# A state-space and expert kernel: the unrolled middle chunks of the first stage become hardware loops

## What is computed

```python
xz = einsum('bld,ed->ble', x, in_proj_w); xi, z = split(xz)          # 512 each
u  = silu(causal_depthwise_conv4(xi) + conv1d_b)
dt_low, B, C = split(einsum('bld,rd->blr', u, x_proj_w))             # 16, 16, 16
delta = softplus(dt_low @ dt_proj_w.T + dt_proj_b)
dA, dBu = exp(delta[..., None] * A), delta[..., None] * B * u[..., None]
h_t = dA_t * h_{t-1} + dBu_t ;  y_t = sum_n h_t[..., n] * C_t[n]     # 16 states
x1 = layernorm(x + ((y + u * D) * silu(z)) @ out_proj_w.T)
# then: softmax router over 8 experts, each expert takes its 2048 best tokens,
# layer norm, two-layer GELU network, weighted scatter-add, and a last layer norm
```

## Time and profile before

| | us |
|---|---|
| three runs | 4682.22, 4683.41, 4690.44; median 4683.41 |
| the profiled execution | 4683.41 |
| its span, first to last instruction | 4681.5 |
| mean granted clock of TensorE, share of full | 0.883 |

### The profile page before, as it was taken

The page is one execution under the profiler, slowest core; times in us unless marked ns, Lnnn a source line. Parts: engine busy times, 40 slices in busy tenths (PEclk is TensorE's granted clock), DMA queues, the critical chain, the costliest instruction groups (busy, mean ns, idle before and its releaser), DMA issues. The chain is left out here.

```text
span 4681.5 us, 57838 instructions
## 1 busy us (share of the span) xinstructions
PE 3739.5 (80%) x19154; PEld 2596.0 (55%) x19154; DVE 3996.9 (85%) x5099; ACT 3393.0 (72%) x5732; POOL 3574.0 (76%) x1744
## 2 busy tenths in 40 slices
PE   7888888888888888888888878888863199999990
PEld 3455555555555555555555555555553178888880
DVE  4999999999999999999999999999994667766645
ACT  5888787888888888878887888888861056555555
POOL 3888888888888888888888888888881156666643
PEclk8889898989888988988898998989875599999995
DMA  2454555554445545545554445545442123333328
GB/s 69 118 127 126 127 125 132 126 127 126 117 122 138 133 120 133 126 117 127 134 130 125 121 119 133 137 122 136 124 112 48 50 46 64 70 60 62 63 33 291
DMA packets 166374, 528.78 MB, mean 113 GB/s; under 512 B 31920, under 2 KB 97584, under 8 KB 118720
## 3 DMA queue, kind: packets, MB, share of 16 engines
q0 software_dynamic: 56832, 268.99, 29.5%
q1 hardware_dynamic: 104640, 239.32, 14.8%
q10 hardware_dynamic: 4608, 16.78, 0.9%
HBM read 221.47 MB, written 68.68 MB: 62 GB/s over the span
## 5 line engine op out<-in xcount | busy, mean ns | idle before, releaser
L369 POOL TENSOR_TENSOR dbu<-du,bb 128x2048 f32<-128x2048 f32 x512 | 2361.8, 4634 | 298.8 <-DVE h L736 274.0
L736 DVE TENSOR_TENSOR_SCAN h<-da,hlast,dbu 128x512 f32<-128x512 f32 x1536 | 1881.4, 1267 | 53.0 <-POOL dbu L369 41.9
L656 PE MATMUL ht<-ident,h 128*128 128x128 f32 x8192 | 1320.7, 308 | 594.6 <-DVE h L736 347.2
L419 ACT ACTIVATE da<-dl,negA 128x512 f32<-128x512 f32 x2048 | 1418.7, 698 | 468.9 <-DVE h L736 463.3
L656 PEld LDWEIGHTS ht<-ident,h 128*128 128x128 f32 x8192 | 1042.5, 157 | 1075.9 <-DVE h L736 555.2
L744 DVE SCALAR_TENSOR_TENSOR pair<-ht,ct,pair 128x512 f32<-128x512 f32 x896 | 639.0, 731 | 85.8 <-PE ht L656 85.4
L736 DVE TENSOR_TENSOR_SCAN h<-da,dbu 128x512 f32<-128x512 f32 x512 | 596.1, 1205 | 39.8 <-ACT da L419 25.0
L442 ACT ACTIVATE pair<-ht,ct 128x512 f32<-128x512 f32 x896 | 591.8, 687 | 50.7 <-PE ht L656 48.4
L589 PE MATMUL spare<-xin,win 128*128 128x512 f32 x1024 | 499.2, 617 | 40.3 <-DMA xin<-in_xt 26.0
L595 PE MATMUL spare<-xh,conv 128*128 128x512 f32 x1024 | 460.8, 592 | 2.2 <-ACT dl L456 1.5
L1149 POOL DMA_INDIRECT sums<-ot,idx x128 | 237.2, 1853 | 172.3 <-DVE ot L1425 130.7
(11 more groups left out here) (162 smaller groups left out, 5688.3 us busy)
## 6 DMA issues: line engine op xcount, KB each, us to landing
acc<-pair POOLq DMA_DIRECT2D x224, 1024.0 KB, 7.1
bb<-b_rows SPq DMA_DIRECT2D x128, 1024.0 KB, 5.2
xin<-in_xt SPq DMA_DIRECT2D x32, 512.0 KB, 4.4
xres<-in_x SPq DMA_DIRECT2D x32, 512.0 KB, 4.1
x_scores<-xres SPq DMA_DIRECT2D x32, 512.0 KB, 5.4
sums<-xres SPq DMA_DIRECT2D x32, 512.0 KB, 7.1
wraw<-in_w SPq DMA_DIRECT2D x16, 1024.0 KB
rows<-sums SPq DMA_DIRECT2D x32, 512.0 KB, 6.3
```

What stands on the lines that cost most here:

```text
L369: pool.tensor_tensor(dbu[n % 2][:], du[q][:], bb[part % 2][:, m:m + 1, :].to_broadcast([P, DT, CH]), ALU.mult).then_inc(dbu_done, 1)
L419: act.activation(da[DA_SLOT[m]][:], dl[q][:, dt, :], ACT.Exp, scale=negA[:, dt, n:n + 1]).then_inc(exp_done, 1)
L656: last = te.transpose(ht[HT_SLOT[m]][:, dt * P:(dt + 1) * P], h[n % 2][:, dt, b * P:(b + 1) * P], ident[:])
L736: dve.tensor_tensor_scan(h[n % 2][:, dt, :], da[DA_SLOT[n * DT + dt]][:], dbu[n % 2][:, dt, :], start, ALU.mult, ALU.add).then_inc(scan_do ...
```

## The change

In each of the five engines' blocks of `stage1` the Python loop over chunks 2 to 29 becomes a hardware loop, `Fori`. On SP, ACT and PE a turn of the loop is two chunks, and there are 14 turns; on POOL and DVE a turn is four chunks, and there are 7. The longer turn is needed since these two treat a sequence's first chunk in another way. Inside the loop the chunk's number is made from the loop's register, so the counts of the waits and the addresses that contain it are computed by register operations when the program runs. No other line changes.

```diff
 # SP (ACT and PE alike)
-                for c in range(2, n_chunks - 2):
-                    chunk(c, c % 2, (FR, P1, P2), True)
+                with sp.Fori(1, n_chunks // 2 - 1) as j:
+                    chunk(2 * j, 0, (FR, P1, P2), True)
+                    chunk(2 * j + 1, 1, (FR, P1, P2), True)
 # POOL (DVE alike)
-                for c in range(2, n_chunks - 2):
-                    chunk(c, c % 4, (FR, P1, P2), True)
+                with pool.Fori(0, n_chunks // 4 - 1) as j:
+                    chunk(4 * j + 2, 2, (FR, P1, P2), True)
+                    chunk(4 * j + 3, 3, (FR, P1, P2), True)
+                    chunk(4 * j + 4, 0, (FR, P1, P2), True)
+                    chunk(4 * j + 5, 1, (FR, P1, P2), True)
```

More of the change, by code:

```diff
@@ L561, in _ @@
                 chunk(1, 1, (FR, P1))
-                for c in range(2, n_chunks - 2):
-                    chunk(c, c % 2, (FR, P1, P2))
+                with act.Fori(1, n_chunks // 2 - 1) as j:
+                    chunk(2 * j, 0, (FR, P1, P2))
+                    chunk(2 * j + 1, 1, (FR, P1, P2))
                 chunk(n_chunks - 2, 0, (FR, P1, P2))
@@ L700, in _ @@
                 chunk(1, 1, (FR, P1), (FR,), True)
-                for c in range(2, n_chunks - 2):
-                    chunk(c, c % 2, (FR, P1, P2), (FR, P1, P2), True)
+                with te.Fori(1, n_chunks // 2 - 1) as j:
+                    chunk(2 * j, 0, (FR, P1, P2), (FR, P1, P2), True)
+                    chunk(2 * j + 1, 1, (FR, P1, P2), (FR, P1, P2), True)
                 chunk(n_chunks - 2, 0, (FR, P1, P2), (FR, P1, P2), False)
@@ L823, in _ @@
                 chunk(1, 1, (FR, P1))
-                for c in range(2, n_chunks - 2):
-                    chunk(c, c % 4, (FR, P1, P2))
+                with dve.Fori(0, n_chunks // 4 - 1) as j:
+                    chunk(4 * j + 2, 2, (FR, P1, P2))
+                    chunk(4 * j + 3, 3, (FR, P1, P2))
+                    chunk(4 * j + 4, 0, (FR, P1, P2))
+                    chunk(4 * j + 5, 1, (FR, P1, P2))
                 chunk(n_chunks - 2, 2, (FR, P1, P2))
```

## The result

The kernel with the loops takes 4820.94 us (median of four runs, 4809.72 to 4828.28) against 4684.05 us before (four runs, 4682.22 to 4690.44). The ratio is 1.0288, with a 95% interval of 1.0264 to 1.0311: 2.9% slower, 137 us. The sign was forecast, the size was not: 4727 us was predicted, and 4821 lies above the range of 4700 to 4785. The profiled execution of the changed kernel took 4813.78 us, its span is 4812.0.

A forecast was written before the change was run, and what follows sets the result against it. The prediction took DVE to bound the kernel and added 38 us for ACT's jumps, 3 for PE's and 3 for registers: 4683.4 + 44 = 4727 us, 0.9% slower. The range was 4700 to 4785 us.

The forecast's parts named there:

- What bounds the kernel: In the state-space stage DVE sets the pace, at 108.5 us a chunk, idling for 6% of it.
- PE's jump: At 13 turn ends PE jumps back, late by 0 to about 1 us and mostly covered: 3 us.
- rival 3: PE's jump at turn ends comes on top of ACT's: 36 us in place of 3, 4760 us; chance 0.13.
- ACT's jump, "the main term": At 13 turn ends a 4.5 us jump delays the first decay, exposing 2.8 or 3.25 us: 38 us.
- lower working: The estimate for ACT's 13 jumps with DVE's 2.9 us in place of 4.5: 17 us.
- DVE's and POOL's jumps: Six each, at turn ends, hidden under ACT's delay: nothing; uncovered, 1.5 us a time for DVE, up to 2.5 for POOL.
- Registers, 3 us: Register operations for waits and addresses in the looped chunks add 0.1 us a chunk, 3 us.
- The equal groups of the expert stage: Four groups there took 100.60 us unrolled, 100.03 and 100.57 looped, taken to show no register cost that can be told.
- the upper bound of 365 us: All some 170 DVE register operations a chunk on the path at about 78 ns: 13 us a chunk.
- rival 4: Register operations stand on DVE's path: a tenth of 365 us gives 4761, a third 4846; above 4790, chance 0.05.
- The sum: Over the looped chunks, ACT's jump 38, PE's jump 3 and registers 3 make 44 us.

The follow-up runs named there:

- padded kernel: The kernel before with the loop on PE alone, plus 12 transposes of the identity (24 instructions) ahead of PE's work: 4707.08 us, ratio 1.0043.
- middle-of-a-block kernel: The changed kernel with 71 transposes (142 instructions) ahead of PE's work, so its loop's head stands mid-block: 4736.51 us, ratio 1.0113 to the kernel before.

## Why the prediction was wrong in size

**What bounds the kernel** was right. DVE's work is unchanged, and what the kernel lost is its idle time.

**PE's jump: the step that failed.** "I take 3 us, as PE may not pay at all and mostly has cover." It did pay, 3.3 to 5.0 us a jump, with 1842 instructions of all kinds in the turn. That it mostly has cover held for the jump alone (20 to 23 us in the padded kernel, registers of PE included). What was missing is the second stop. The target is 14 instructions ahead of a packet's end, PE uses them up in its fifth transpose, and stands for 1.9 to 6.5 us before the next. This is rival 3's way (PE late, passed on whole) with another size: it had 2.8 us a jump, 36 in all, and PE measured 81 to 86 alone and 96 to 101 within the change (4821 against 4725). In the expert stage PE stood for 2.55 us where the group took 4.0 us longer; the prediction noted that this was not all of it, and did not follow it further. PE does not stop a second time there, so that loop could not have shown what was missing.

The Trainium skill (Runtime: NRT & Kernel Launch, Instruction fetch mechanics) says that the stream comes in 16 KiB blocks, fetched in sequence ahead of use, and that crossing a block's boundary is mostly hidden. PE's packets here have that size, those of q14 have 1.94 MB / 238 = 8 KB. Hidden it was in the unrolled kernel, where no transpose of PE is behind a stop of "issue", and not behind a jump, where 5.68 us were seen. The page also gives PE's memory for instructions as 2048 of them, though it speaks of a window of two blocks beside it; the body of 1842 was not held, as each of the 13 jumps took 3.3 us and more. It is the measurement that decides here.

**Why the next packet is late** is in part argued. In the changed kernel three of PE's packets start around the first jump (branch at 507.3): at 508.0, 508.4 and 516.5 us. I take the first for the sequential successor of the loop's end, which is of no use after the jump, and the second for the target. The loop's end lies some 36 instructions into a packet, so that the fetch ahead and the jump can meet. At the six jumps without such an extra packet the next one starts 0.7 to 1.5 us behind the branch's end, and PE goes on 2.2 to 3.3 us after that start. So it comes only once the target runs, and 14 instructions do not last that long. Seven of the 13 jumps have the extra packet. In five of them it starts at most 0.9 us ahead of the target's, and these are the five longest second stops, 5.68 to 6.50 us; the other two have 2.35 and 3.46, and the six jumps without one 1.87 to 3.07. In the five the awaited packet starts 4.4 to 5.1 us behind the branch's end. So the second stop is there with and without the extra packet, and long where the two start together. In the middle-of-a-block kernel, where the loop's end lies elsewhere too, there is no such packet and its jumps are 3.3 to 3.9 us. Two kernels moved the loop's end alone, by another length of the turn: with turns of four the end is some 86 instructions into a packet and the six second stops are 2.25 to 2.86 us, with turns of twelve it is 15 to 30 into one, the two packets start 0.4 us apart, and the one second stop is 5.39 us. So the head's place brings the stop, and the end's place seems to decide whether it is a long one; the head was never moved alone.

**How ACT passes it on** is read from the timelines: its product waits 5.84 us for the tile and the decays stand behind it. That the wait comes with PE's loop and goes with its second stop is shown (DVE's waits on `da` 84.8 us with PE's loop alone, 29.9 with it padded, 23.2 before). That putting decays ahead of that product would save the time wasn't tried. Beside this, PE's clock was at its lower level for the stretch: 0.51 from 514 to 524 us against 1.00 from 500 to 514. It fell while PE stood, and eleven transposes behind the stop took 2.50 us where twelve took 1.47 at 526 us.

```profile
500.00:514.00 14.00, 8.94 (x35) 4.51 (x34) 10.66 (x12) 7.97 (x15) 9.22 (x4) 1.00 0.59 121
514.00:524.00 10.00, 5.16 (x15) 3.60 (x15) 3.02 (x3) 4.32 (x9) 3.16 (x2) 0.51 0.28 57
```

That makes the second stop's harm somewhat larger than its length; how much of it was not separated.

**ACT's jump, "the main term".** The mechanism was right, where it was said to be: a decay late at a turn's first scan. The term of 38 us was mis-sized, by taking 4.5 us from the expert stage. The jump took 2.5 to 3.6 us here, DVE's waits for a decay at the turns' first scans are 23.6 us in the changed kernel, and ACT's loop alone cost 13 to 15 us. The prediction's lower working, 17 us with 2.9 us a jump, was near.

**DVE's and POOL's jumps, nothing as they lie under ACT's.** POOL's 6 us alone fits nothing to little. DVE's loop measured 30 alone, of which some 16 are registers, so 14 for six jumps without cover, or 11 by the idle time at their scans; 9 were said. Within the change they cannot be told from the rest.

**Registers, 3 us.** They are about 27, 1 us a chunk. The equal groups of the expert stage were a poor witness, as the prediction half said: PE was the bound there, so DVE's spare time can have taken them up. A tenth of the upper bound of 365 us (rival 4) was nearer than 0.1 us a chunk.

**The sum.** By the single parts: PE 81 to 86, DVE 30, ACT 13 to 15, POOL 6. Seen by kinds: about 27 of registers, 60 to 77 of PE's second stop, and the rest, 33 to 50, the jumps of four engines. 44 us were forecast, and that is near what the change costs once PE's head is moved (52 to 54 us), though by a different make-up: that nearness would have been luck.

None of these kernels is faster than the unrolled one.

## What to carry to other kernels

Price a hardware loop for each engine as jumps times what each exposes, and count every kind of instruction in the body: here bodies of 379 and more instructions paid for the jump, and one of some 160 in the expert stage's loop did not. Look where the loop's first instruction stands in the instruction stream: with few instructions left in its block the engine stops twice for each jump, which a few instructions of padding cured here, and fewer and longer turns helped too. And where an in-order engine is named in a wait, ask what it was itself waiting for: here most of "DVE waits for ACT" was PE's lack of instructions.

## What the runs showed of the hardware

- A jump back took 2.4 to 3.9 us on ACT, DVE and POOL with bodies of 391 to 1038 instructions, and 3.3 to 5.0 us on PE with 1842 (up to 5.7 with the loop on PE alone). SP with 57 went on after 0.24 to 0.29 us, and POOL in the expert stage (160) after 0.3. What a jump takes is not what it costs: DVE lost 1.2 us for each of ACT's.
- A second stop of 1.9 to 6.5 us followed when the jump's target was 14 instructions ahead of its 16 KB packet's end (5.1 to 6.5 us where two packets started less than 1 us apart around the jump); with 246 left, or about half, there was none.
- Register operations cost about 1 us for a chunk of 108 us where DVE was the bound (two turns of 12), and the expert stage showed nothing.
- A hardware loop of one turn left nearly no register operations: 57853 instructions against 57838.
